# Cosine attention over chunks as a pipeline, and ternary weights made on GpSimd during the next layer's expert loop

## The chip, the cores and the metric

One core of a Trainium2 chip runs the whole program: TensorE (PE), VectorE (DVE), ScalarE (ACT), GpSimd (POOL), and SyncE (SP), which here only issues DMAs. The metric is the device time of one execution in microseconds. The engines run their own instruction lists and meet only at semaphores.

## What is computed

The program is four layers, each an attention-like sublayer and a feed-forward sublayer, over `x` of 8 x 256 tokens with 256 features, and a context of 8 x 256 tokens with 192 features. The change touches the first two sublayers and the preparation of weights for two later ones.

```
# layer 0, cosine attention: added to x
v = layernorm(x) @ Wv.T + bv            # 128 features per token
t = ctx @ Wt.T + bt
x = x + (v . t) / max(|v| * |t|, 1e-8)  # 256 x 256 for each of 8 batches

# layer 0, experts: 2 shared and 16 routed, the 4 most probable of each token gated
x = x + sum_e gate_e * (gelu(layernorm(x) @ up_e.T) @ down_e.T)

# ternary weights of layer 1 (3 matrices) and layer 3 (7 matrices)
s = max(mean|W|, 1e-5);  q = (W > s/2) - (W < -s/2)      # -1, 0 or 1
```

## The kernel before

The residual `X` stays in SBUF as 16 tiles of 128 tokens x 256 features. The cosine sublayer `l0_cosine` works in NC = 4 chunks of 512 tokens (TPC = 4 tiles, two batches). Before its loop, `layernorm` turns the normalised tokens into `XT`.

In a chunk, TensorE projects both sides into PSUM banks 0 and 1 (L494 to L496). ScalarE writes from them the squares `sq` (L527, L528) and the sides `vT`, `tT` (L529, L530). TensorE sums the squares over features by sixteen one-column instructions (L503, the squared lengths), ScalarE takes the root, VectorE the reciprocal `rn` (L541). TensorE spreads the reciprocal lengths over rows (L510) and makes the products v . t (L514). VectorE multiplies and limits the reciprocals (`lim`, L548), multiplies by the products (`cos`, L553), adds to `X` (L557) and takes the statistics of the new `X` (L156). Every one of `sq`, `vT`, `tT`, `norm`, `rn`, `lim` and `cos` is one buffer, so the order within a chunk is a chain: the lengths wait for all four of ScalarE's outputs, and the reciprocal of the next chunk stands on VectorE behind all work of the chunk before.

Into the same loop `TernaryWeights` is put, in three groups (`GROUPS`: matrices 0 and 1; 2 to 7; 8 and 9), one to each of the first three chunks. All ten matrices lie side by side in `tern_w`, 128 x 14336 fp32. ScalarE sums the absolute values (L404), TensorE spreads the sums over partitions (L409), VectorE makes the scales and thresholds (L417 to L422), GpSimd compares with the lower threshold into `below` (L427; VectorE does it for the largest matrix, `OWN = 8`), and VectorE makes `q` from the weights and `below` by one instruction per matrix (`high`, L441), in the chunk after, between the reciprocal and `lim`. SyncE stores `q` to DRAM.

The feed-forward sublayer `l0_ffn` follows. Each `nc.Block()` ends with a barrier of all engines. Its `layernorm` loads the router's weights and the attention weights of layer 1 into `K.raw` (128 x 8192 fp32, allocated after the cosine sublayer). Its `router` (L616 to L653) makes logits on TensorE; ScalarE copies `XT` to `XH` rounded, GpSimd subtracts to get `XL` (L632); VectorE then has a chain of softmax and top-4 up to the gates (L642 to L653), with the exponentials on ScalarE (L625). `small_experts` loops over 18 experts in pairs. GpSimd splits each expert's weights into a high and a low part (L725 to L729), as soon as the expert before the last is done (two buffers). A unit is an expert and a chunk, four units per expert: TensorE makes the hidden values (L744), ScalarE the gelu (L768) and its rounded copy `h_hi` (L771), VectorE the rest `h_lo` (L782), which reads two SBUF tensors, TensorE the outputs in 12 matmuls (L755 to L757), VectorE adds them gated to `X` in 4 instructions (L789), which read one tensor in PSUM and one in SBUF. TensorE runs the hidden values of the next unit ahead of the outputs of this one.

Of the kernel before, what the change touches and what calls it, by code (L numbers as in the profile page):

```python
# [26 lines left out]
ds = bass.ds  # L27

P = 128
# [332 lines left out]
class TernaryWeights:  # L362

    GROUPS = [(0, 2), (2, 8), (8, 10)]
    OWN = 8

    def __init__(self, K, ctx):
        nc, n = K.nc, TERNARY_AT[-1]
        self.K = K
        self.w = ctx.enter_context(nc.sbuf_tensor("tern_w", [P, n], F32))
        self.below, self.q = (ctx.enter_context(nc.sbuf_tensor("tern_" + x, [P, n], BF16)) for x in ("below", "q"))
        self.sums, self.thr = (ctx.enter_context(nc.sbuf_tensor("tern_" + x, [P, w], F32)) for x, w in (("sums", len(TERNARY)), ("thr", 2 * len(TERNARY))))
        self.loaded = [K.sem(f"tern_loaded{i}") for i in range(len(TERNARY))]  # L380
        self.zeroed, self.summed, self.total, self.thr_ok, self.below_ok, self.q_ok, self.stored = (
            K.sem("tern_" + x) for x in ("zeroed", "summed", "total", "thr", "below", "q", "stored"))

    def part(self, t, i):
        return t[:, TERNARY_AT[i]:TERNARY_AT[i + 1]]

    def zero_missing_rows(self, dve):

        for i, (_, rows, cols) in enumerate(TERNARY):
            if rows % P:  # L390
                dve.memset(self.w[rows % P:P, TERNARY_AT[i + 1] - cols:TERNARY_AT[i + 1]], 0.0).then_inc(self.zeroed, 1)

    def load(self, sp):
        for i, (name, rows, cols) in enumerate(TERNARY):
            load_rows(sp, self.part(self.w, i).rearrange("p (k n) -> p k n", n=cols), self.K.a[name], self.loaded[i])

    def sum(self, act, g):
        for i in range(*self.GROUPS[g]):
# [5 lines left out]
            act.activation(self.part(self.below, i), self.part(self.w, i), ACT.Abs, accum_out=self.sums[:, i:i + 1]).then_inc(self.summed, 1)  # L404

    def spread(self, pe, g):
        a, b = self.GROUPS[g]
        pe.wait_ge(self.summed, b)
        pe.matmul(self.K.bank[6][:, a:b], self.K.ones[:], self.sums[:, a:b], start=True, stop=True).then_inc(self.total, 1)  # L409

    def scales(self, dve, g):
        K, o = self.K, self.K.dve_order
        dve.wait_ge(self.total, g + 1)
        span = range(*self.GROUPS[g])
        for i in span:
            count = TERNARY[i][1] * TERNARY[i][2]
            o.mark(dve.tensor_scalar(K.wscale[:, i:i + 1], K.bank[6][:, i:i + 1], 1.0 / count, 1e-5, ALU.mult, ALU.max))  # L417
        o.wait(dve)
        a, b = self.GROUPS[g]
        n = len(TERNARY)  # L420
        dve.tensor_scalar(self.thr[:, a:b], K.wscale[:, a:b], 0.5, None, ALU.mult).then_inc(self.thr_ok, 1)
        dve.tensor_scalar(self.thr[:, n + a:n + b], K.wscale[:, a:b], -0.5, None, ALU.mult).then_inc(self.thr_ok, 1)  # L422

    def compare_low(self, eng, i, g):
        eng.wait_ge(self.thr_ok, 2 * (g + 1))
        n = len(TERNARY)
        return eng.tensor_scalar(self.part(self.below, i), self.part(self.w, i), self.thr[:, n + i:n + i + 1], None, ALU.is_lt)  # L427

    def low(self, pool, g):
        for i in range(*self.GROUPS[g]):  # L430
            if i != self.OWN:
                self.compare_low(pool, i, g).then_inc(self.below_ok, 1)

    def high(self, dve, g):
        o = self.K.dve_order
        for i in range(*self.GROUPS[g]):
            if i == self.OWN:
                o.step(dve, self.compare_low(dve, i, g))
            else:
                dve.wait_ge(self.below_ok, i + 1 - (i > self.OWN))  # L440
            dve.scalar_tensor_tensor(self.part(self.q, i), self.part(self.w, i), self.thr[:, i:i + 1], self.part(self.below, i),  # L441
                                     ALU.is_gt, ALU.subtract).then_inc(self.q_ok, 1)

    def store(self, sp):
        pieces = [(0, 2), (2, 8), (8, 9), (9, 10)]
        for a, b in pieces:
            sp.wait_ge(self.q_ok, b)
            w = slice(TERNARY_AT[a], TERNARY_AT[b])
            sp.dma_start(self.K.qweights[:, w], self.q[:, w]).then_inc(self.stored, 16)
        sp.wait_ge(self.stored, 16 * len(pieces))  # L450
# [3 lines left out]
def l0_cosine(K):  # L454
# [4 lines left out]
    nc, a, X, XT, CT, bank = K.nc, K.a, K.X, K.XT, K.CT, K.bank  # L459
    HV = 128  # L460
    with ExitStack() as ctx:
# [3 lines left out]
        vT, tT, sq = sb("vT", [P, CH]), sb("tT", [P, CH]), sb("sq", [P, 2, CH])  # L465
        norm, rn, lim, cos = sb("norm", [P, 2 * TPC]), sb("rn", [P, 2 * TPC]), sb("lim", [P, TPC, S]), sb("cos", [P, TPC, S])
# [10 lines left out]
        ternary = TernaryWeights(K, ctx)  # L477
        with nc.Block() as block:
# [5 lines left out]
        proj, sides, norms, roots, recips, dots, added = (  # L484
            K.sem("l0x_" + n) for n in ("proj", "sides", "norms", "roots", "recips", "dots", "added"))
        assert len(ternary.GROUPS) == NC - 1
        with nc.Block() as block:
            @block.tensor
            def _(pe):
                for c in range(NC):  # L490
# [8 lines left out]
                    pe.wait_ge(sides, 4 * c + 4)  # L499
# [2067 lines left out]
```

## Time and profile before

| | |
|---|---|
| median of 3 runs | 1811.87 us (1810.94 to 1814.45) |
| the profiled execution | 1816.25 us, span 1814.5 us |
| mean granted TensorE clock | 0.901 |
| busy: PE, DVE, ACT, POOL | 82%, 57%, 44%, 27% of the span |
| cosine chunks (27.1 to 106.4 us) | 79.3 us |
| layernorm and router of `l0_ffn` (106.4 to 138.1 us) | 31.7 us |
| expert loop (138.1 to 357.4 us) | 219.3 us |
| the later five sublayers | the rest, about 1457 us |

Times in the trace count from the start of the span. PEclk is the granted clock, 1.00 at 2.4 GHz and 0.50 at 1.2 GHz. A busy share over the whole span says little here, as sublayers with different limits follow each other behind barriers; the stretch has to be read.

### The profile page before, as it was taken

How to read it: one execution, taken by the hardware profiler on the slowest of the kernel's cores; microseconds unless marked ns; L12 is line 12 of the kernel's file. 1: busy time of each engine (PE TensorE's matmuls, PEld its weight loads, DVE VectorE, ACT ScalarE, POOL GpSimd, SP SyncE). 2: the span in 40 equal slices, each digit the busy share in tenths (PEclk: the TensorE clock that was granted, in tenths of full speed). 3: DMA queues.
4: the chain of work that ended last, by engine and by line, in shares of the span. 5: the costliest groups of instructions: out<-in, count | busy, mean ns of one | idle time of the engine just before them, and what ended most of it. 6: DMA issues, size and time to landing. Idle time of an engine off the chain costs nothing. (4 is left out here: it accounts for less than half of the span.)

```text
span 1814.5 us, 28465 instructions
## 1 busy us (share of the span) xinstructions
PE 1480.9 (82%) x8632; PEld 1094.7 (60%) x8632; DVE 1032.7 (57%) x2508; ACT 805.3 (44%) x1905; POOL 485.8 (27%) x717
## 2 busy tenths in 40 slices
PE   4648999789999999556599986865567739999997
PEld 3537888667777777423477764541343527667665
DVE  3766888865555555578666655545666523333332
ACT  3223444465555555456555544325546612332331
POOL 0532222263333433100264420000000442222222
PEclk9668999989999999889799999955888759999999
DMA  7141000019500000000000000013000651111110
GB/s 258 47 128 35 23 23 23 4 36 290 128 1 1 1 1 1 35 0 0 3 1 1 1 1 23 1 50 139 1 0 1 222 197 42 48 48 50 46 47 6
DMA packets 64019, 89.26 MB, mean 49 GB/s; under 512 B 7056, under 2 KB 55072, under 8 KB 62880
## 3 DMA queue, kind: packets, MB, share of 16 engines
q1 hardware_dynamic: 58624, 75.08, 13.5%
q0 software_dynamic: 5280, 12.74, 2.1%
q8 instruction: 61, 1.00, 0.2%
q14 instruction: 54, 0.44, 0.1%
HBM read 56.09 MB, written 33.54 MB: 49 GB/s over the span
## 5 line engine op out<-in xcount | busy, mean ns | idle before, releaser
L1218 POOL TENSOR_SCALAR XT<-XT,l1x_rs 128x256 f32<-128x256 f32 x256 | 117.8, 479 | 191.0 <-DVE l1x_rs L1130 191.0
L1134 DVE TENSOR_REDUCE l1x_nmax<-bank 128x2 f32<-128x512 f32 x128 | 87.4, 684 | 110.5 <-PE bank L982 110.5
L1075 ACT ACTIVATE XT<-bank,l1x_nmax 128x256 f32<-128x256 f32 x256 | 118.7, 471 | 68.5 <-DVE l1x_nmax L1134 68.5
L2227 PE MATMUL bank<-l3x_wu,XT 128*128 x312 | 142.6, 601 | 0.8 <-ACT XT L2261 0.6
L2236 PE MATMUL bank<-l3x_wd,CT 128*128 x624 | 141.4, 380 | 1.7 <-DVE CT L2304 1.6
L994 PE MATMUL bank<-ident,XT 128*128 128x128 f32 x768 | 120.7, 280 | 8.9 <-POOL XT L1218 3.3
L2236 PEld LDWEIGHTS bank<-l3x_wd,CT 128*128 128x128 f32 x624 | 115.9, 191 | 16.5 <-issue 2.6
L789 DVE SCALAR_TENSOR_TENSOR X<-bank,l0f_gates,X 128x256 f32<-128x256 f32 x288 | 118.9, 474 | 0.0
L994 PEld LDWEIGHTS bank<-ident,XT 128*128 128x128 f32 x768 | 84.3, 140 | 42.6 <-POOL XT L1218 23.6
L2271 ACT ACTIVATE CT<-bank,l3x_b 128x128 f32<-128x128 f32 x156 | 44.5, 368 | 139.3 <-PE bank L2245 139.3
L1141 DVE COPY l1x_pt<-bank 128x512 f32<-128x512 f32 x128 | 87.8, 686 | 30.2 <-PE bank L994 30.2
L2227 PEld LDWEIGHTS bank<-l3x_wu,XT 128*128 128x128 f32 x312 | 57.2, 193 | 58.4 <-issue 58.4
L768 ACT ACTIVATE l0e_h<-bank 128x512 f32<-128x512 f32 x72 | 43.0, 598 | 109.5 <-PE bank L744 109.5
L755 PE MATMUL bank<-l0e_wdhi,l0e_hhi 128*128 128x256 f32 x288 | 82.5, 287 | 2.1 <-DVE l0e_hlo L782 1.9
L782 DVE TENSOR_TENSOR l0e_hlo<-l0e_h,l0e_hhi 128x512 fp32r<-128x512 f32 x72 | 58.3, 810 | 42.7 <-ACT l0e_hhi L771 42.2
L757 PE MATMUL bank<-l0e_wdhi,l0e_hlo 128*128 128x256 f32 x288 | 81.7, 284 | 0.0
L756 PE MATMUL bank<-l0e_wdlo,l0e_hhi 128*128 128x256 f32 x288 | 81.7, 284 | 0.0
L1218 POOL TENSOR_SCALAR XT<-XT,l2x_rs 128x256 f32<-128x256 f32 x128 | 58.9, 479 | 79.3 <-DVE l2x_rs L1130 79.2
L2212 POOL DMA_INDIRECT out_x<-XT x39 | 39.2, 1005 | 144.8 <-DVE XT L2291 144.8
L2287 DVE TENSOR_TENSOR XT<-bank,CT 128x256 f32<-128x256 f32 x39 | 16.6, 425 | 103.6 <-PE bank L2236 103.6
L2296 DVE COPY CT<-bank 128x512 f32<-128x512 f32 x39 | 27.0, 692 | 84.1 <-PE bank L2227 84.1
L1075 ACT ACTIVATE XT<-bank,l2x_nmax 128x256 f32<-128x256 f32 x128 | 59.3, 471 | 33.8 <-DVE l2x_nmax L1134 33.8
(517 smaller groups left out, 3892.0 us busy)
## 6 DMA issues: line engine op xcount, KB each, us to landing
slots<-blank SPq DMA_DIRECT2D x9, 1987.5 KB, 22.8
l3x_wu<-in_L_ffn_W SPq DMA_DIRECT2D x8, 1024.0 KB
l3x_wd<-in_L_ffn_W SPq DMA_DIRECT2D x8, 1024.0 KB
XT<-slots SPq DMA_DIRECT2D x39, 132.5 KB, 2.1
qweights<-tern_q SPq DMA_DIRECT2D x3, 1024.0 KB, 3.9
l0e_wu<-in_L_ffn_upT SPq DMA_DIRECT2D x18, 128.0 KB, 2.1
l0e_wd<-in_L_ffn_downT SPq DMA_DIRECT2D x18, 128.0 KB, 2.1
X<-in_x SPq DMA_DIRECT2D x1, 2048.0 KB, 8.2
```

Of the source, the lines that this page charges most:

```text
L755: pe.matmul(y, h_hi[:, c % 2, w], wd_r[s][0][:], start=True, stop=False)
L756: pe.matmul(y, h_hi[:, c % 2, w], wd_r[s][1][:], start=False, stop=False)
L757: last = pe.matmul(y, h_lo[:, c % 2, w], wd_r[s][0][:], start=False, stop=True)
L782: dve.tensor_tensor(h_lo[:, c % 2, :], h[:, c % 2, :], h_hi[:, c % 2, :].bitcast(F32), ALU.subtract).then_inc(lo_done, 1)
L789: dve.scalar_tensor_tensor(X[:, t, :], YB[c % 2 * 2 + j // 2][:, j % 2 * D:(j % 2 + 1) * D], gates(t, pair * 2 + s), X[:, t, :], ALU.mult, ...
L994: last = pe.transpose(tp[:, c:c + P], pr[n % 3][:, i, q, kt * P:(kt + 1) * P], K.ident[:])
L1075: act.activation(pr[n % 3][:, i, q, :], sc[(2 * n + i) % 3][:, q * S:(q + 1) * S], ACT.Exp, bias=nmax[:, n % 3, i, q:q + 1], accum_out=sum ...
L1134: dve.tensor_reduce(nmax[:, n % 3, i, :], sc[(2 * n + i) % 3][:].rearrange("p (q s) -> p q s", q=QT), AX, ALU.max, negate=True).then_inc(m ...
L1141: dve.tensor_copy(pt[n % 2][:, i, :], tp[:]).then_inc(pt_ok, 1)
L1218: pool.tensor_scalar(t, t, rs[:, n % 3, i, q:q + 1], 1.0, ALU.mult, ALU.mult).then_inc(norm_ok, 1)
L2227: last = pe.matmul(up_b[half][:], xT[:, k, :], wu[:, ds(e * KD + k, 1), half * CH:(half + 1) * CH].rearrange("p a n -> p (a n)"), start=k ...
L2236: last = pe.matmul(y_b[:, 0:D], hT[:, m, :], wd[:, ds(e * HT + m, 1), :].rearrange("p a n -> p (a n)"), start=m == 0, stop=m == HT - 1)
```

## The change

`l0_cosine` becomes a pipeline: two buffers for `vT`, `tT`, `sq`, `norm`, `rn` and `cos`, products in banks 4 to 7 in turn, and on TensorE the projection of chunk c+1 before the products of chunk c, and the lengths of chunk c+1 behind them. The lengths wait for the two squares only. VectorE multiplies and adds two tiles at a time, and takes the statistics of a chunk after the next chunk's adds.

Of the ternary work only the sums of the first eight matrices (`FRONT = 8`) stay on ScalarE in this loop, with their scales at its end. Their raw weights now lie in `K.raw` (128 x 8192), the last two matrices' in `tern_back`. The comparisons are cut into 14 pieces of 1024 columns. Pieces 0 and 1 (`AHEAD = 2`) are made in `router`, the lower comparison on GpSimd before `XL`, `high` on VectorE before the logits. The other twelve are made on GpSimd alone, in three steps each (lower comparison, upper comparison, subtraction), 36 steps spread over the experts 1 to 17. The sums of the last two matrices go to ScalarE in `router`, their scales to the start of `small_experts`. The load of layer 1's attention weights and the stores of `q` go behind SyncE's expert loop.

```diff
 class TernaryWeights:
...
+    FRONT = 8
+    PIECE = 1024
+    AHEAD = 2
...
+    def low(self, pool, piece):
...
+        for i, lo, hi in self.parts(piece):
+            pool.wait_ge(self.thr_ok, 2 * (self.FRONT if i < self.FRONT else n))
+            pool.tensor_scalar(self.q[:, lo:hi], self.raw(lo, hi), self.thr[:, n + i:n + i + 1], None, ALU.is_lt).then_inc(self.below_ok, 1)
...
+    def high(self, dve, piece):
+        dve.wait_ge(self.below_ok, self.done(piece + 1))
+        for i, lo, hi in self.parts(piece):
+            dve.scalar_tensor_tensor(self.q[:, lo:hi], self.raw(lo, hi), self.thr[:, i:i + 1], self.q[:, lo:hi],
                                      ALU.is_gt, ALU.subtract).then_inc(self.q_ok, 1)
 
+    def compare_high(self, pool, piece):
+        pool.wait_ge(self.q_ok, self.done(piece))
+        for i, lo, hi in self.parts(piece):
+            start = piece * self.PIECE
+            pool.tensor_scalar(self.above[:, lo - start:hi - start], self.raw(lo, hi), self.thr[:, i:i + 1], None, ALU.is_gt).then_inc(self.above_ok, 1)
+
+    def combine(self, pool, piece):
...
+        pool.tensor_tensor(self.q[:, w], self.above[:], self.q[:, w], ALU.subtract).then_inc(self.q_ok, self.done(piece + 1) - self.done(piece))
...
+    def steps(self):
+        return 3 * (TERNARY_AT[-1] // self.PIECE - self.AHEAD)
...
@@ l0_cosine, TensorE
+                def lengths(c):
+                    pe.wait_ge(sides, 4 * c + 2)
...
+                def products(c):
                     pe.wait_ge(recips, c + 1)
                     if c:
+                        pe.wait_ge(limited, TPC * c)
...
+                project(0)
+                lengths(0)
+                for c in range(NC):
+                    if c + 1 < NC:
+                        project(c + 1)
+                    products(c)
+                    if c + 1 < NC:
+                        lengths(c + 1)
+                pe.wait_ge(roots, NC)
+                ternary.spread(pe, 0, ternary.FRONT)
...
@@ l0_cosine, ScalarE
                     if c:
+                        ternary.sum(act, c - 1, c)
...
+                ternary.sum(act, NC - 1, ternary.FRONT)
...
@@ l0_cosine, VectorE
                 for c in range(NC):
+                    dve.wait_ge(dots, c + 1)
...
+                        dve.tensor_scalar(lim[:, j, :], bank[3][:, j // 2 * S:(j // 2 + 1) * S], rn[:, c % 2, j:j + 1],
+                                          1.0 / COS_EPS, ALU.mult, ALU.min).then_inc(limited, 1)
...
+                        dve.tensor_tensor(cos[:, c % 2, 2 * b:2 * b + 2, :], bank[4 + c % 2 * 2 + b][:].rearrange("p (i s) -> p i s", s=S),
+                                          lim[:, 2 * b:2 * b + 2, :], ALU.mult).then_inc(cos_ok, 1)
+                    if c + 1 < NC:
+                        recip(c + 1)
...
+                        dve.tensor_tensor(xt, xt, cos[:, c % 2, 2 * b:2 * b + 2, :], ALU.add).then_inc(added, 1)
+                    if c:
+                        stats(c - 1)
+                ternary.scales(dve, 0, ternary.FRONT)
+                stats(NC - 1)
...
@@ router
+                if ternary:
+                    ternary.sum(act, ternary.FRONT, len(TERNARY))
...
+                    if ternary:
+                        for piece in range(ternary.AHEAD):
+                            ternary.low(pool, piece)
...
+                if ternary:
+                    for piece in range(ternary.AHEAD):
+                        ternary.high(dve, piece)
...
@@ small_experts
+                sp.wait_ge(ternary.q_ok, ternary.done(8))
+                if K.last >= 2:
+                    load_attention_weights(K, sp, "l1x")
+                ternary.store(sp)
...
-                for s in range(2):
-                    split(0, s)
-                with pool.Fori(1, E // 2) as pair:
-                    for s in range(2):
-                        split(pair, s)
+                for e in range(E):
+                    split(e)
+                    if e:
+                        for n in range((e - 1) * ternary.steps() // (E - 1), e * ternary.steps() // (E - 1)):
+                            ternary.step(pool, n)
```

## Rows read from the trace of the kernel before

**Rows 1.** Windows: stretch, length, busy PE, PEld, DVE, ACT, POOL, granted clock, DMA

```profile
27.00:31.10 4.10, 3.87 (x8) 1.35 (x8) 0.00 (x0) 3.98 (x5) 0.00 (x0) 1.00 1.07 384
48.10:51.80 3.70, 3.57 (x16) 3.49 (x16) 0.00 (x1) 0.05 (x1) 3.59 (x1) 0.50 0.01 4
57.70:61.60 3.90, 3.84 (x9) 1.30 (x9) 3.90 (x2) 0.02 (x1) 1.38 (x1) 1.00 0.01 2
90.00:106.40 16.40, 2.75 (x10) 1.99 (x8) 16.24 (x19) 0.00 (x0) 5.72 (x1) 0.60 0.23 96
119.00:138.10 19.10, 10.76 (x64) 10.68 (x64) 7.28 (x60) 5.41 (x4) 8.99 (x2) 0.59 0.23 63
149.80:348.00 198.20, 198.07 (x1259) 177.65 (x1257) 166.77 (x351) 94.68 (x148) 51.73 (x64) 1.00 0.06 19
```

**Rows 2.** Timeline, cosine chunks on PE and ACT: start, length, engine, line, operation

```profile
37.45 2.07 PE L510 MATMUL bank<-ident,l0x_rn 128*128 128x128 f32 x8 [0.50 <-DVE l0x_rn L541]
39.31 2.47 PE L514 MATMUL bank<-l0x_tT,l0x_vT 128*128 128x256 f32 x8
48.14 3.57 PE L503 MATMUL bank<-ones,l0x_sq 128*128 128x1 f32 x16 [2.51 <-ACT l0x_tT L530]
54.09 3.60 PE L514 MATMUL bank<-l0x_tT,l0x_vT 128*128 128x256 f32 x8
61.58 0.69 ACT L527 ACTIVATE l0x_sq<-bank,l0x_bv 128x512 f32<-128x512 f32 x1 [4.17 <-PE bank L496]
```

**Rows 3.** Timeline, VectorE in the last chunk

```profile
88.07 2.35 DVE L427 TENSOR_SCALAR tern_below<-tern_w,tern_thr 128x4096 bf16<-128x4096 f32 x1
...
90.46 10.07 DVE L441 SCALAR_TENSOR_TENSOR tern_q<-tern_w,tern_thr,tern_below 128x4096 bf16<-128x4096 f32 x2
100.46 1.65 DVE L548 TENSOR_SCALAR l0x_lim<-bank,l0x_rn 128x256 f32<-128x256 f32 x4
102.14 1.42 DVE L553 TENSOR_TENSOR l0x_cos<-bank,l0x_lim 128x256 f32<-128x256 f32 x4
103.59 1.43 DVE L557 TENSOR_TENSOR X<-X,l0x_cos 128x256 f32<-128x256 f32 x4
104.94 1.40 DVE L156 BATCH_NORM_STATS2 stats<-X 128x6 f32<-128x256 f32 x4
```

**Rows 4.** Timelines, ternary comparisons of VectorE and GpSimd side by side

```profile
53.69 5.81 DVE L441 SCALAR_TENSOR_TENSOR tern_q<-tern_w,tern_thr,tern_below 128x2048 bf16<-128x2048 f32 x1 [1.52 <-POOL tern_below L427]
53.65 5.43 POOL L427 TENSOR_SCALAR tern_below<-tern_w,tern_thr 128x2048 bf16<-128x2048 f32 x1
59.42 2.34 DVE L441 SCALAR_TENSOR_TENSOR tern_q<-tern_w,tern_thr,tern_below 128x2048 bf16<-128x2048 f32 x1
78.03 1.17 DVE L441 SCALAR_TENSOR_TENSOR tern_q<-tern_w,tern_thr,tern_below 128x512 bf16<-128x512 f32 x1 [0.37 <-POOL tern_below L427]
77.97 1.56 POOL L427 TENSOR_SCALAR tern_below<-tern_w,tern_thr 128x512 bf16<-128x512 f32 x1
```

**Rows 5.** Router: GpSimd's second subtraction, VectorE's first with two SBUF inputs

```profile
125.50 4.51 POOL L632 TENSOR_TENSOR l0f_xl<-XT,l0f_xh 128x2048 fp32r<-128x2048 f32 x1
130.75 0.42 DVE L646 TENSOR_TENSOR l0r_ex<-l0r_lg,l0r_mx 128x256 f32<-128x256 f32 x1
```

**Rows 6.** Timelines, expert loop, GpSimd and VectorE

```profile
182.15 1.10 POOL L725 TENSOR_TENSOR l0e_wuhi<-l0e_wu,zero 128x256 fp32r<-128x256 f32 x1 [8.03 <-PE bank L757]
184.72 0.74 POOL L729 TENSOR_TENSOR l0e_wdlo<-l0e_wd,l0e_wdhi 128x256 fp32r<-128x256 f32 x1
184.79 1.22 DVE L782 TENSOR_TENSOR l0e_hlo<-l0e_h,l0e_hhi 128x512 fp32r<-128x512 f32 x1 [0.56 <-ACT l0e_hhi L771]
187.61 0.69 DVE L782 TENSOR_TENSOR l0e_hlo<-l0e_h,l0e_hhi 128x512 fp32r<-128x512 f32 x1
329.48 1.10 POOL L725 TENSOR_TENSOR l0e_wuhi<-l0e_wu,zero 128x256 fp32r<-128x256 f32 x1 [8.03 <-PE bank L757]
```

**Rows 7.** Groups of 27 to 107 us: ScalarE's sum of the largest matrix

```profile
L404 ACT ACTIVATE tern_below<-tern_w 128x4096 bf16<-128x4096 f32 x1 | 3.6, 3608 | 0.0
```

More of the change, by code:

```diff
@@ L424, in compare_low @@
[L424 to L441, printed above, removed]
-                                     ALU.is_gt, ALU.subtract).then_inc(self.q_ok, 1)
+            w = slice(TERNARY_AT[i], TERNARY_AT[i + 1])
@@ L444, in store, with step @@
+    def step(self, pool, n):
+        piece = self.AHEAD + n // 3
+        if n % 3 == 0:
+            self.low(pool, piece)
+        elif n % 3 == 1:
+            self.compare_high(pool, piece)
+        else:
+            self.combine(pool, piece)
+    def steps(self):
+        return 3 * (TERNARY_AT[-1] // self.PIECE - self.AHEAD)
     def store(self, sp):
[L445 to L448, printed above, removed]
+        for a, b in ((0, 8), (8, 14)):
+            sp.wait_ge(self.q_ok, self.done(b))
+            w = slice(a * self.PIECE, b * self.PIECE)
@@ L489, in _, with project @@
             def _(pe):
-                for c in range(NC):
+                def project(c):
                     if c:
@@ L561, in _ @@
-                    if c < NC - 1:
-                        ternary.scales(dve, c)
-            @block.gpsimd
-            def _(pool):
-                for g in range(NC - 1):
-                    ternary.low(pool, g)
-            @block.sync
-            def _(sp):
-                ternary.store(sp)
+                        dve.tensor_scalar(lim[:, j, :], bank[3][:, j // 2 * S:(j // 2 + 1) * S], rn[:, c % 2, j:j + 1],
+                                          1.0 / COS_EPS, ALU.mult, ALU.min).then_inc(limited, 1)
@@ L777, in _ @@
                 dve.sem_inc(lo_done, 2)
+                ternary.scales(dve, ternary.FRONT, len(TERNARY))
                 def rest(pair, s, c, n):
@@ L2502, in _ @@
                     sp.wait_ge(K.ctx_loaded, 48)
-        for sublayer in stages[first:min(last + 1, 1)]:
-            sublayer(K)
         with nc.sbuf_tensor("raw", [P, 8 * 1024], F32) as raw:
             K.raw = raw
-            for sublayer in stages[max(first, 1):min(last + 1, 5)]:
+            with ExitStack() as weights:
+                K.ternary = TernaryWeights(K, weights)
+                for sublayer in stages[first:min(last + 1, 2)]:
+                    sublayer(K)
+            for sublayer in stages[max(first, 2):min(last + 1, 5)]:
                 sublayer(K)
```

171 lines of the change are left out of this document (90 added, 81 removed).

## The prediction

> **What bounds the kernel now.** The barriers between sublayers make the whole span's shares useless, so I first read windows cut at the barriers and phases [rows 1]. They show three regimes. In the cosine chunks nothing is busy throughout: in 27.00:31.10 TensorE projects and VectorE has nothing, in 90.00:106.40 VectorE works for 16.24 of 16.40 us and TensorE for 2.75. In the router every engine mostly waits for one chain. In the expert loop TensorE is busy for 198.07 of 198.20 us at a clock of 1.00, and VectorE for 166.77. So a microsecond on VectorE is worth one in the first, and nothing in the loop until its spare (16%) is gone.
>
> The timeline then tells the order inside a chunk [rows 2, 3]: projection, squares, lengths, reciprocal, products, VectorE. In the last chunk the products have long been possible when VectorE is still on ternary weights: 88.07 to 100.46, 12.4 us, and only then `lim`. The stage ends at 104.94 + 1.40 = 106.3.
>
> **Cosine, what sets the end after.** VectorE loses all comparisons and keeps per chunk 1.65 + 1.42 + 1.43 + 1.40 = 5.9 us and a reciprocal [rows 3]. TensorE needs more, so I sum along it [rows 1, 2]. A projection takes 3.9 us (3.84 to 3.87 busy, at clock 1.00). Lengths take 3.6 at half clock (3.57), which I round to 3.5, since the clock may be higher. Products take 39.31 - 37.45 = 1.9 for the spreading, and 2.5 (clock rising) to 3.6 (half) for the rest: 4.4 to 5.5. The first projection still ends at 31.0; two squares of at most 0.7 each free the lengths at 32.3 (before, they waited for four outputs); lengths end at 35.8. Three rounds of projection, products and lengths follow, then 0.5 for root and reciprocal (the idle before L510), and the last products. With 4.4: 35.8 + 3 x 11.8 + 0.5 + 4.4 = 76.1. With 5.5: 35.8 + 3 x 12.9 + 0.5 + 5.5 = 80.5. If the three later projections ran wholly at the half clock they'd take 3.9 more each: 92.2. No row shows a projection that follows lengths directly; the clock was 0.50 during lengths at 48.10 and 1.00 in the projection behind products at 57.70. I take 79, for some of each.
>
> Behind the last products VectorE has `lim`, `cos`, add, the third chunk's statistics, the scales and the fourth's statistics. That is 1.65 + 1.42 + 1.43 + 2 x 1.40 = 7.3 [rows 3], and the ten scale instructions on a few columns. Their nearest row is 0.42 for 256 columns [rows 5], which bounds them by 0 and 4.2; they are hundreds of times smaller, so near the low end: 0.7. Two tiles per instruction save at most two starts each. Tail 8.0, end 87.0. ScalarE's work per chunk (four outputs, one sum) lies under TensorE's 12 us, and the last sums (matrices 3 to 7, together half of the largest one's 3.6 us, and four more starts [rows 7]) beside the last products. Gain 106.3 - 87.0 = **19.3 us**, between 23 (76.1 + 7.3) and 5.5 (92.2 + 8.6).
>
> **Router.** Put before `XL` on GpSimd: two comparisons of 1024 columns. 512 columns took 1.56 us and 2048 took 5.43 [rows 4], 2.52 ns per column and 0.27 fixed, so 2.85 each, 5.7 together. They start at the block's start, 119.0. Behind them `XL` is 2 x 4.5 [rows 5], so GpSimd ends at 133.7 and not at 130.0. VectorE's two `high` (half of 2.34 each, 1.2, alone) lie under its wait for the logits at 129.8, if they are let in. But VectorE's chain then has L646 at 130.75, with two SBUF inputs, where GpSimd's second subtraction used to be over and now runs. How two such instructions meet the trace shows [rows 4, 6]: whoever started first goes on, and the other gains little. VectorE's `h_lo` at 184.79, behind L729 at 184.72, takes 1.22 instead of 0.69; GpSimd's L725 takes 1.10 behind an `h_lo`. L729 held the other for 0.53 of its 0.74 us, a two-input instruction for 0.7 to all of its length. So L646 waits until 133.3 to 133.7, or to 135 where a `high` has got between the subtractions: +2.2 to +4. The bound below is 0 (it gets in before the second subtraction). I take **+3.2**. ScalarE's added sums (3.6 [rows 7] and half of it, 5.4) hide: it is busy 5.41 us in that window [rows 1], and 10.8 in all still fits before the exponential at 131.2. The start of the next block moves with this chain; the spread and scales there lie under the wait for the first weights.
>
> **Expert loop.** GpSimd's added work: twelve pieces, two comparisons of 2.85 and a subtraction. A two-input one is 4.51 for 2048 columns, 0.74 for 256 [rows 5, 6], so 2.4. That is 97 us, with 1.6 for pieces 6 and 7, which are cut at the matrices' borders: 99 us over 17 experts, 5.8 each. An expert takes (329.48 - 182.15) / 13 = 11.33 us, and GpSimd waits for 8.03 of them [rows 6]. It fits. Two gaps have three steps, 8.1; what they run over is taken from the split's double buffer, needed a whole expert later. So GpSimd is no bound.
>
> What counts is `h_lo`, the only VectorE instruction of the loop with two SBUF inputs (the adds, L789, read one). VectorE has 11.33 x 0.16 = 1.8 us spare per expert, 0.45 per unit, and one `h_lo` of four already takes 0.53 longer with TensorE still full [rows 1, 6]. A comparison holds the other engine for only part of its time: behind one of 512 columns a VectorE instruction took 1.17 where 0.6 is its own, +0.55 of 1.56; behind one of 2048, 5.81 and not 2.34, +3.5 of 5.43 [rows 4]. For 1024 that makes 1.3 to 1.7 from the step's start. Counted from the split's start at 182.15, `h_lo` comes at 2.6, 5.5 and 8.3; the first step starts at 3.3 to 3.8, the second near 6.7. So `h_lo` arrives 1.6 to 2 us into a step and finds the way free or nearly so; behind a subtraction (held for 1.7 of 2.4) it waits 0.2 to 0.4. That stays within 0.45. I take 0.1 per expert, **+1.5**; bounds 0, and the rival below.
>
> The Trainium skill speaks against this part: "SBUF — State Buffer", section Who interferes with whom, says that the one which starts second is fully blocked until the first has finished. The trace disagrees with it in size: by that rule the instruction at 53.69 would have taken 5.4 + 2.3 = 7.7 us, and took 5.81 [rows 4]. What the rule would make of the loop is rival B.
>
> **Hidden moves.** Layer 1's weights and the stores now stand behind SyncE's loop. Its last expert load follows the split of expert 15, about two experts before 329.48, so near 310; the 4.2 MB of `raw` at the 384 GB/s of the first window are 11 us, landed by 322, and attention starts after 357. GpSimd's last three steps end at 329.5 + 3.3 + 8.1 = 341, and the last store (1.5 MB, 4 us) near 345, while TensorE is still busy at 348 [rows 1, 6]. Nothing; without that cover it would cost what exceeds 357.
>
> **Sum.** -19.3 + 3.2 + 1.5 = -14.6 us. The profiled execution took 1816.25 (span 1814.5 and 1.75 around it), which gives 1801.65; the median of the runs is 4.4 below that execution, so **1797 us** for a median. The forecast's own range is 1793 to 1804.
>
> **Rivals.**
> A, the clock. The one-column lengths keep TensorE at 1.2 GHz through each projection. For it: the lengths of 48.10:51.80 ran at 0.50. Against: TensorE no longer idles, and the projection of 57.70:61.60 was at 1.00 right behind products [rows 1]. End of the stage at 92.2 + 8 = 100.2, gain 6.1, net -1.4: 1810.5.
> B, the opposite side: `h_lo` waits to the end of each GpSimd step. Steps at 3.8 to 6.65 and 7.3 to 10.2 delay the `h_lo` at 5.5 and 8.9 by 1.2 and 1.3. Per expert that is 2.5 less two spares of 0.45, 1.6; or, if VectorE makes use of all its spare, 2.5 - 1.8 = 0.7. The middle, 1.15 x 17 = 19.6, with +4.5 in the router: net +4.8, 1816.7. It decides from (19.3 - 4.5) / 17 = 0.87 us per expert. For it: the skill's rule, and the `h_lo` at 184.79, held for most of L729 [rows 6]. Against: 5.81 where the rule makes 7.7 [rows 4].
> C, more gain: TensorE at full clock throughout and L646 not held: -23 + 0 + 0.5, 1789.4.
>
> **Chances.** The forecast 0.74, A 0.08, B 0.10, C 0.08. A change under 0.2%, 3.6 us, can't be told from none in this kernel. A lies within it; B is slower in a bit over half of its cases, the others are faster. Faster 0.84, same 0.09, slower 0.07. The range of 1791 to 1809 leaves out B's upper part, half of C and little else.
>
> **What would show it.** Cosine chunks ending near 87 (over 95: clock or a wait I missed), with TensorE busy throughout 36 to 75; VectorE without L441's kind there; projections of 3.9. L646 of 3 us or more in the router, and GpSimd's subtractions up to 134. In the loop 11.3 to 11.5 us per expert, and `h_lo` with a mean under 1.1 us (before, 1.22 once per expert and 0.69 otherwise [rows 6]); a mean over 1.5, and TensorE waiting for it, means B. Attention's start waiting for `raw` would be a cost that I put at nothing. The prediction is wrong if the stage's order on TensorE leaves gaps: each is paid four times.

## The result, and the profile after

The changed kernel takes 1785.83 us (median of 4 executions, 1784.32 to 1787.35) against 1811.4 of the kernel before in the same comparison (1810.43 to 1814.45): a ratio of 0.9842, 95% interval 0.982 to 0.9864. It is 25.6 us faster; 14.6 were forecast. A later comparison on one chip gave 1786.96 against 1809.94, ratio 0.9872 (0.9851 to 0.9893), so the gain is 23 to 26 us. Either time lies beyond the low end of the predicted range, 1791.

The profiled execution took 1784.32 us, with a span of 1782.6 and a mean granted clock of 0.911. First its windows, cut as in [rows 1]: one whole round of the pipeline, the end of the cosine stage, the router, the expert loop.

```profile
core 0: us, PE busy (x) PEld busy (x) DVE busy (x) ACT busy (x) POOL busy (x), PEclk, DMA share, GB/s
45.80:54.00 8.20, 8.20 (x42) 5.52 (x41) 4.09 (x10) 4.46 (x8) 0.00 (x0) 1.00 0.01 2
62.40:76.00 13.60, 4.69 (x19) 4.03 (x18) 11.25 (x36) 2.81 (x11) 0.00 (x0) 0.69 0.00 1
76.70:110.70 34.00, 17.07 (x96) 16.14 (x96) 24.52 (x85) 15.69 (x17) 15.75 (x5) 0.60 0.01 1
110.70:332.90 222.20, 208.25 (x1298) 185.39 (x1298) 183.01 (x382) 99.04 (x153) 161.29 (x115) 0.96 0.17 57
```

The first row is what the change is about: in the cosine stage TensorE is now busy for all of a round, at a clock of 1.00, and VectorE for half of it. Where a chunk before went through 3.57 us of lengths at half clock [rows 1], TensorE's timeline of the changed kernel shows this (L510 to L512 project, L522 the lengths, L530 and L537 the products):

```profile
start us, us, engine line op out<-in xcount [idle before <-releaser]
32.46 2.61 PE L522 MATMUL bank<-ones,l0x_sq 128*128 128x1 f32 x16 [1.36 <-ACT l0x_sq L559]
34.94 3.76 PE L510 MATMUL bank<-XT,l0x_wv 128*128 128x512 f32 x4
...
41.39 1.16 PE L530 MATMUL bank<-ident,l0x_rn 128*128 128x128 f32 x8
42.38 1.89 PE L537 MATMUL bank<-l0x_tT,l0x_vT 128*128 128x256 f32 x8
44.11 1.84 PE L522 MATMUL bank<-ones,l0x_sq 128*128 128x1 f32 x16
...
60.58 1.84 PE L522 MATMUL bank<-ones,l0x_sq 128*128 128x1 f32 x16
63.80 1.67 PE L530 MATMUL bank<-ident,l0x_rn 128*128 128x128 f32 x8 [1.38 <-DVE l0x_rn L577]
65.26 3.09 PE L537 MATMUL bank<-l0x_tT,l0x_vT 128*128 128x256 f32 x8
```

The reader is to see two things. The same sixteen one-column instructions that took 3.57 us take 1.84, and the eight instructions of the products 1.89, not 3.60 [rows 2]. And the engine is slow again in just two places, each behind a wait: after 1.36 us of idle time the lengths take 2.61 and the next projection 6.45 (34.94 to 41.39, at a granted clock of 0.58) for its usual 3.9, and after 1.38 us the last products take 3.09. (The profile shows each fp32 matmul of the program as two instructions: e4's three extra matmuls appear as x6.)

VectorE's end of the stage, and then its part of the router with GpSimd's instructions beside it:

```profile
63.55 0.19 DVE L577 RECIPROCAL l0x_rn<-l0x_norm 128x8 f32<-128x8 f32 x1
...
68.39 1.66 DVE L590 TENSOR_SCALAR l0x_lim<-bank,l0x_rn 128x256 f32<-128x256 f32 x4 [2.17 <-PE bank L537]
...
74.53 1.40 DVE L156 BATCH_NORM_STATS2 stats<-X 128x6 f32<-128x256 f32 x4
...
94.25 5.55 DVE L434 SCALAR_TENSOR_TENSOR tern_q<-raw,tern_thr,tern_q 128x1024 bf16<-128x1024 f32 x1 [0.69 <-POOL tern_q L429]
...
100.63 3.81 DVE L689 TENSOR_TENSOR l0r_ex<-l0r_lg,l0r_mx 128x256 f32<-128x256 f32 x1
```
```profile
88.54 5.68 POOL L429 TENSOR_SCALAR tern_q<-raw,tern_thr 128x1024 bf16<-128x1024 f32 x2 [0.42 <-SPq L646]
94.19 9.97 POOL L672 TENSOR_TENSOR l0f_xl<-XT,l0f_xh 128x2048 fp32r<-128x2048 f32 x2
```

The stage ends at 75.93, and not at 106.3. In the router L434 (the second `high`) came 0.06 us behind the start of the first subtraction of L672 and got through only after that had ended (98.7); the second subtraction (5.47 us of the two's 9.97) then ran to 94.19 + 9.97 = 104.16, and L689, which was L646 and took 0.42 [rows 5], came while it ran and ended at 104.44.

Then the groups of the expert loop, 110.7 to 332.9, and below them the group of `h_lo` before:

```profile
line engine op names shapes xcount | busy us, mean ns | idle before us <-releasers
L830 DVE TENSOR_TENSOR l0e_hlo<-l0e_h,l0e_hhi 128x512 fp32r<-128x512 f32 x72 | 63.7, 885 | 36.6 <-ACT l0e_hhi L818 36.4
...
L801 PEld LDWEIGHTS bank<-l0e_wdhi,l0e_hhi 128*128 128x128 f32 x288 | 54.8, 190 | 9.9 <-DVE l0e_hlo L830 4.5 <-issue 2.9
...
L447 POOL TENSOR_TENSOR tern_q<-tern_above,tern_q 128x1024 bf16<-128x1024 bf16 x12 | 28.0, 2337 | 1.1 <-POOL tern_above L441 0.2
```
```profile
L782 DVE TENSOR_TENSOR l0e_hlo<-l0e_h,l0e_hhi 128x512 fp32r<-128x512 f32 x72 | 58.3, 810 | 42.7 <-ACT l0e_hhi L771 42.2
```

`h_lo` has a mean of 885 ns and had 810 before, 5.4 us in the whole loop. VectorE still stands idle for 36.6 us ahead of it, and TensorE's weight loads wait for it for 4.5 us (3.5 before).

By the starts of the sublayers (VectorE's first statistics instruction) the two profiled executions compare so:

| | before | after | part's difference |
|---|---|---|---|
| `l0_ffn` starts | 107.3 | 76.7 | -30.6 (cosine) |
| gates made (L653, now L696) | 137.4 | 110.7 | +3.9 (layernorm, router) |
| layer 1 attention starts | 358.5 | 332.9 | +1.1 (loop) |
| layer 2 feed-forward starts | 1094.2 | 1069.0 | +0.4 |
| layer 3 attention starts | 1210.2 | 1180.0 | -5.0 |
| end of the span | 1814.5 | 1782.6 | -1.7 |

Up to layer 1 this is -25.6, the whole difference of the medians in the first comparison (23.0 in the later one). The last two rows are code that the change doesn't touch. They are what one execution differs from another there: a second profiled execution of the changed kernel had layer 2's feed-forward part at 1066.7 to 1182.8, 116.1 us, where the first had 111.0 and the kernel before 116.0. So the sum has to be read up to layer 1.

### The profile page after: what moved, and what is told of

Read it like the earlier page. It is cut to its first block and busy times, and to the rows that moved or that the text cites. A ratio compares the mean times of both kernels' runs of the same rounds, so it can differ in the third digit from the quotient of the medians.

```text
span 1782.6 us, 28456 instructions
## 1 busy us (share of the span) xinstructions
PE 1464.7 (82%) x8630; PEld 1079.6 (61%) x8630; DVE 1019.5 (57%) x2481; ACT 805.4 (45%) x1905; POOL 565.0 (32%) x752
## 5 line engine op out<-in xcount | busy, mean ns | idle before, releaser
L830 DVE TENSOR_TENSOR l0e_hlo<-l0e_h,l0e_hhi 128x512 fp32r<-128x512 f32 x72 | 63.7, 885 | 36.6 <-ACT l0e_hhi L818 36.4
L2256 POOL DMA_INDIRECT XT<-out_x,XT x39 | 40.5, 1039 | 104.6 <-DMA out_x<-XT 95.8
## 6 DMA issues: line engine op xcount, KB each, us to landing
tern_back<-in_L_xattn_W_f1T SPq DMA_DIRECT2D x1, 2048.0 KB, 10.7
```

What stands on the lines that cost most here:

```text
L830: dve.tensor_tensor(h_lo[:, c % 2, :], h[:, c % 2, :], h_hi[:, c % 2, :].bitcast(F32), ALU.subtract).then_inc(lo_done, 1)
```

## The experiments

Two theories of the 11 us that the cosine stage gained beyond the forecast stood against each other. The clock theory: the times of the lengths and products before were half-clock times, and the clock was half because the old order let TensorE wait; without the waits they halve. The neighbour theory: TensorE's short instructions were slowed by the ternary work that ran beside them on VectorE and GpSimd. And of GpSimd's steps in the expert loop it was open whether they cost little because they hold VectorE only in part, or because the schedule kept them apart. E5 to e8 ran on a chip on which the kernel before took 1823.62 us (e1 to e4: 1812.47; e9 to e11: 1809.94), so ratios are compared, or differences within a trace.

**E1, the old order of the chunks, with the ternary work moved.** `l0_cosine` keeps its old loop and single buffers; the ternary work is where the change puts it.

```diff
-                    pe.wait_ge(sides, 4 * c + 2)
+                    pe.wait_ge(sides, 4 * c + 4)
...
-                project(0)
-                lengths(0)
```


> The changed kernel with the old chunk loop (single buffers, the lengths behind all four outputs, one tile per add), and the ternary work moved as in the change. Theory 1, the clock: what made the cosine stage 11 us shorter than predicted is that TensorE, kept busy by the pipeline, ran the lengths and products at 2.4 GHz (lengths 1.7 us, products 2.6 us per chunk, where I had priced 3.5 and 4.4 to 5.5 from half-clock rows). Then here, with TensorE idle between steps, the lengths still take about 3.4 us and the products 4.4 or more, a chunk 14.7 us, and the stage ends near 93 us (75.9 in the changed kernel): total 1803 us. Rival, theory 2, the neighbours: they took long because VectorE and GpSimd worked on the ternary weights beside them. Then lengths are at 1.8 and products at 2.7 here too, a chunk takes 12 us, the stage ends near 82 us: total 1792 us.

Measured 1800.9 us, ratio 0.9938 (0.9907 to 0.9969). Its timeline of TensorE in the second chunk (L517 the lengths, L524 and L528 the products), and the windows of lengths and products:

```profile
46.61 3.58 PE L517 MATMUL bank<-ones,l0x_sq 128*128 128x1 f32 x16 [2.51 <-ACT l0x_tT L543]
50.69 2.07 PE L524 MATMUL bank<-ident,l0x_rn 128*128 128x128 f32 x8 [0.50 <-DVE l0x_rn L555]
52.56 3.62 PE L528 MATMUL bank<-l0x_tT,l0x_vT 128*128 128x256 f32 x8
```
```profile
46.60:50.20 3.60, 3.58 (x16) 3.49 (x16) 0.00 (x0) 0.00 (x0) 0.00 (x0) 0.50 0.00 0
50.70:56.00 5.30, 5.30 (x17) 4.58 (x18) 0.00 (x0) 1.59 (x2) 0.00 (x0) 0.50 0.01 3
```

VectorE and GpSimd show 0.00 in both rows, and the lengths still take 3.58 and the products 3.62 at a clock of 0.50. The neighbour theory falls. The waits of 2.51 and 0.50 us stand in front of the slow instructions. The clock doesn't always fall within such a wait: in the first chunk the lengths behind the same 2.51 us took 1.95, at 0.97, and only the spreading behind them was slow (2.08).

**E2, the pipeline, with the ternary work where it was.** The other half of the change alone, built on the kernel before: the new loop, with the old `TernaryWeights` in it (the diff is against the kernel before). Its sums move from bank 6, which the products now need, to bank 2 of the lengths, so the lengths also wait for the thresholds.

```diff
-        pe.matmul(self.K.bank[6][:, a:b], self.K.ones[:], self.sums[:, a:b], start=True, stop=True).then_inc(self.total, 1)
+        pe.matmul(self.K.bank[2][:, 16 + a:16 + b], self.K.ones[:], self.sums[:, a:b], start=True, stop=True).then_inc(self.total, 1)
...
+                def lengths(c):
+                    pe.wait_ge(sides, 4 * c + 2)
...
+                    pe.wait_ge(ternary.thr_ok, 2 * max(c, 1))
```


> The kernel before with the pipelined chunk loop and nothing of the ternary work moved (three groups, on ScalarE, GpSimd and VectorE in the cosine stage; the sums spread one place earlier, since bank 2 is shared with the lengths). VectorE then has 23 us of cosine and 28 us of ternary work from about 43 us on, with waits for GpSimd between: the stage ends at 92 to 98 us, 8 to 14 us before the old one, total 1798 to 1803. If the two parts of the change were independent, this and the run with the old loop would add up to the whole 25.6 us; I expect them to fall short of it by 4 us or more, since each alone leaves the other's chain as the bound. Theory 1: the lengths are near 2 us wherever TensorE has not waited, 3.4 behind a wait. Theory 2: they stay above 3 us, as the ternary work is beside them.

Measured 1798.9 us, ratio 0.9932 (0.9905 to 0.9958). It answers the two theories from the other side. The lengths at 50.91 took 1.84 us at a clock of 1.00, with GpSimd on its ternary comparison for all of that time (1.70 of 1.70 us in 50.91:52.61); the last ones, behind a wait of 4.45 us for the thresholds, took 2.75. Layer 0's feed-forward part starts at 95.8 (-11.5). The medians' two halves are 11.6 and 13.6 us, 25.2 together and near the whole's 25.6, but each has an interval of some 10 us from end to end. The traces, up to layer 1, are sharper: -9.0 (349.5 for 358.5) and -10.7 (347.8), 19.7 together for 25.6, as the expectation said (4 us or more short). In the cosine stage alone the halves give 13.3 and 11.5 of the 30.6. So the two help each other by 6 us there: without the moved ternary work VectorE is the bound (busy almost without a gap from 57.4 to 93.2), and without the pipeline TensorE's waits are. How much of the 6 us is due to this run's added wait for the thresholds isn't separated.

**E3, no pieces in the router.** All 14 pieces are made in the expert loop.

```diff
-    AHEAD = 2
+    AHEAD = 0
```


> The changed kernel with AHEAD = 0: all 14 pieces in the expert loop, none in the router. The router's 3.7 us are, by my prediction's step, VectorE's L689 waiting for GpSimd's second subtraction (3.81 us, 0.42 before). Then L689 falls back to 0.42 and the router by 3.4 us; the loop has 42 steps for 36, GpSimd about 10.5 of 11.33 us busy per expert, and pays 0 to 0.5 us: total 1782.5 us. Rival: the subtraction isn't what holds it, and the total stays at 1786; or GpSimd gets past 11.33 us per expert and the loop is 5 us or more longer, total 1788 or more.

Measured 1782.8 us as the median of four (one took 2056.96; the other three have a median of 1781.73), ratio 0.9827 (0.9788 to 0.9865) without that one. The interval overlaps the changed kernel's, so the gain is read from the trace:

```profile
98.75 0.43 DVE L689 TENSOR_TENSOR l0r_ex<-l0r_lg,l0r_mx 128x256 f32<-128x256 f32 x1
```

L689 takes 0.43 us again, and from the start of the part to the gates there are 30.1 us, as before the change; the loop took 221.7 with six more steps. So the two pieces account for the router's +3.9, of which 3.4 are L689. The length of this part also varies by itself: e7 and e11, likewise without pieces, took 32.5 and 31.2, with logits of 13.0 and 12.1 us where e3 has 10.7.

**E4, filler that keeps TensorE busy in the two waits.** Three extra matmuls of 256 columns ahead of the first lengths and of the last products, into banks that nothing reads.

```diff
                 project(0)
+                warm(7, 3)
                 lengths(0)
...
+                    else:
+                        pe.wait_ge(sides, 4 * NC)
+                        warm(0, 3)
```


> The changed kernel with three fp32 matmuls of 256 columns on data that is there, before the first lengths (TensorE waits 1.36 us there) and before the last products (1.38 us); their results are used by nothing. Theory 1: the wait before the first lengths brings the clock down, so that the second projection takes 6.45 us instead of 3.8, and the wait before the last products stretches these (4.2 for 2.6 us). Filled, both run at the full clock: 2.6 and 1.4 us less, total 1782 us. Theory 2, or a clock that falls for another reason (the lengths themselves): nothing gained, 1786 us.

Measured 1780.64 us, ratio 0.9824 (0.9786 to 0.9863). That interval too overlaps the changed kernel's; the trace is sharper. Its timeline of TensorE (L542 is the filler), and the windows over the first two projections and over the second filler with the last products:

```profile
31.70 1.56 PE L542 MATMUL bank<-XT,ident 128*128 128x256 f32 x6
33.12 1.95 PE L522 MATMUL bank<-ones,l0x_sq 128*128 128x1 f32 x16
34.93 1.96 PE L510 MATMUL bank<-XT,l0x_wv 128*128 128x512 f32 x4
...
61.14 1.16 PE L530 MATMUL bank<-ident,l0x_rn 128*128 128x128 f32 x8
62.14 1.89 PE L537 MATMUL bank<-l0x_tT,l0x_vT 128*128 128x256 f32 x8
```
```profile
27.90:45.00 17.10, 17.09 (x75) 10.62 (x76) 3.54 (x9) 7.08 (x12) 0.00 (x0) 1.00 0.46 178
59.60:64.00 4.40, 4.40 (x26) 3.71 (x25) 3.96 (x10) 2.83 (x12) 0.00 (x0) 1.00 0.01 2
```

With the waits filled, the second projection takes 3.8 us and not 6.45, the last products 1.89 and not 3.09, and the clock is 1.00 in both windows. From the first projection to the next part there are 44.5 us, where the changed kernel has 49.5: 2.6 from the projection, 0.7 from the first lengths and 1.7 from the last spreading and products. The same work on the same data became faster by giving the engine more to do.

**E5, larger pieces.** Pieces of 2048 columns, one of them in the router; 6 in the loop, 18 steps of about twice the length.

```diff
-    PIECE = 1024
-    AHEAD = 2
+    PIECE = 2048
+    AHEAD = 1
```


> The changed kernel with pieces of 2048 columns (one in the router, six in the expert loop, 18 steps over 17 experts). It asks how long a GpSimd comparison holds a VectorE instruction with two SBUF inputs. Theory hold: for part of its length, 0.55 us at 512 columns, 3.5 at 2048. Each h_lo that falls into the first 3.5 us of a 5.4 us step is then late by 1 to 3 us, more than the 0.45 us per unit that VectorE has to spare; one or two of the four per expert do. The mean of h_lo rises from 0.89 to 1.3 us or more, the loop by 0.5 to 1 us per expert, 9 to 17 us: total 1794 to 1803. Rival: it is not the length of the instruction that counts (a fair split between the two engines): the same GpSimd time costs the same, h_lo stays near 0.9 and the total at 1786. The router has the same columns before XL, so 3 to 4 us as in the changed kernel.

Measured 1820.06 us, ratio 0.9977 (0.9958 to 0.9997). The loop takes 249.4 us, 27.2 more than with pieces of 1024, and `h_lo` 92.7 us in all where it took 63.7. The timelines of GpSimd and, below, of VectorE's `h_lo` show how:

```profile
153.06 4.55 POOL L447 TENSOR_TENSOR tern_q<-tern_above,tern_q 128x2048 bf16<-128x2048 bf16 x1
...
166.12 5.88 POOL L429 TENSOR_SCALAR tern_q<-raw,tern_thr 128x2048 bf16<-128x2048 f32 x1
```
```profile
155.24 2.92 DVE L830 TENSOR_TENSOR l0e_hlo<-l0e_h,l0e_hhi 128x512 fp32r<-128x512 f32 x1
...
168.28 2.54 DVE L830 TENSOR_TENSOR l0e_hlo<-l0e_h,l0e_hhi 128x512 fp32r<-128x512 f32 x1
```

An `h_lo` takes 0.69 alone. The one at 155.24 ended at 158.16, so it was let in at about 157.5, as the two-input L447 ended (157.61). The one at 168.28 ended at 170.82 and was let in at about 170.1, 4.0 us into a comparison of 5.88. So the partial hold that the prediction read off the comparisons is real, as is the full one of two-input instructions. The cost is 1.6 us per expert, and well over what was expected. It comes through `h_lo`: TensorE's weight loads waited for it for 27.1 us (4.5 in the changed kernel), while GpSimd itself still had 3.5 to 5.3 us to spare per expert in the stretch shown. The same total of GpSimd work costs little in 36 steps of about 3 us (1.7 us, e6) and takes the change's gain away in 18 of 4.5 to 6.

The Trainium skill ("SBUF — State Buffer", section Who interferes with whom) has the second instruction fully blocked for the whole of the first. For the two-input L447 this trace agrees (let in at 157.5, end 157.61); for the comparison it doesn't (let in 1.9 us before its end).

**E6, no steps in the loop.** The 36 steps are left out, so the ternary values of pieces 2 to 13 are not computed.

```diff
-                        for n in range((e - 1) * ternary.steps() // (E - 1), e * ternary.steps() // (E - 1)):
-                            ternary.step(pool, n)
+                        pass
+                pool.sem_inc(ternary.q_ok, ternary.done(14) - ternary.done(ternary.AHEAD))
```


> The changed kernel with the 36 steps left out of the expert loop: the ternary values of pieces 2 to 13 are not computed, and later layers read what lay there; the same number of instructions follows. It prices the steps. By my prediction they cost 1.5 us, by the trace of the changed kernel the loop is 1.1 us longer than before: total 1784.7, h_lo back to a mean of 0.81. Rival B (h_lo held to the end of each step) would have them cost 20 us; then 1766.

Measured 1799.05 us, ratio 0.9847 (0.9808 to 0.9887). The loop takes 220.5 us and `h_lo` has a mean of 812 ns, as before the change:

```profile
L830 DVE TENSOR_TENSOR l0e_hlo<-l0e_h,l0e_hhi 128x512 fp32r<-128x512 f32 x72 | 58.4, 812 | 40.3 <-ACT l0e_hhi L818 40.0
```

So the steps cost 1.7 us in the loop (one execution each; the loop before the change, without steps too, took 221.1), and rival B's 19.6 are refuted. The ratio, too, is the changed kernel's within its interval.

**E7, both improvements together.** `AHEAD = 0` and the filler.

> The version that the runs so far point to: the changed kernel with all pieces in the expert loop and the fillers before the first lengths and the last products. If the two gains are of separate stages they add: -4.4 in router and loop, -5 in the cosine stage, total 1776.5 us. Rival: GpSimd at 10.6 of 11.33 us per expert leaves no room, or the clock comes down later instead; then 1780.

Measured 1789.8 us, ratio 0.9807 (0.9771 to 0.9843). On the scale of 1811.9 that is 1776.9, as expected, but the interval is 13 us wide; in the trace attention of layer 1 starts at 325.6, 7.3 us earlier than in the changed kernel and not 8.9. E11 repeats it.

**E8, the old order with filler.** As e1, with six matmuls of 256 columns between the projection and the lengths of every chunk. If the waits make the clock fall, filling them must help the old order too.

```diff
+                    warm(pe, 6)
                     pe.wait_ge(sides, 4 * c + 4)
```


> The run with the old chunk loop and the ternary work moved, with six fp32 matmuls of 256 columns in each chunk between projection and lengths, where TensorE waits 2.5 us for ScalarE; nothing else is overlapped. Theory 1, the clock: filled, the lengths take 1.8 us and the products 2.6 in all four chunks (3.5 and 4.4 to 5.5 in three of four without filler), so the stage ends some 9 to 12 us sooner, at 81 to 84 us where it was 93.2: total 1789 to 1792. Theory 2, that the pipeline's order makes them cheap and not the clock: the stage stays at 93, total 1801.

Measured 1803.59 us, ratio 0.9883 (0.9846 to 0.992). TensorE in its first two chunks behind the filler (L521 lengths, L528 and L532 products):

```profile
33.73 1.84 PE L521 MATMUL bank<-ones,l0x_sq 128*128 128x1 f32 x16
36.08 1.16 PE L528 MATMUL bank<-ident,l0x_rn 128*128 128x128 f32 x8 [0.51 <-DVE l0x_rn L559]
37.07 3.33 PE L532 MATMUL bank<-l0x_tT,l0x_vT 128*128 128x256 f32 x8
...
46.91 1.84 PE L521 MATMUL bank<-ones,l0x_sq 128*128 128x1 f32 x16
49.25 1.16 PE L528 MATMUL bank<-ident,l0x_rn 128*128 128x128 f32 x8 [0.50 <-DVE l0x_rn L559]
50.25 1.89 PE L532 MATMUL bank<-l0x_tT,l0x_vT 128*128 128x256 f32 x8
```

The lengths take 1.84 in all four chunks, with no other change; the stage is 7.9 us shorter than in e1. Summed over the chunks the lengths give 4.8 us, the spreading 3.2 and the products 0.6; the projections and the fillers' own ends take 0.7 back. It is less than the 9 to 12 expected, because the products fell to half clock all the same in three of four chunks (3.33, 3.14, 3.58). That they didn't in the second, behind the same idle time of 0.50, is not explained by these runs.

**E9, filler in the router too.** E7, and more. The transposes of the layernorm (6.65 us in e7) and the router's logits (13.02) run mostly at half clock. Four fillers stand ahead of the transposes, four among the logits.

```diff
+                    if ternary and t % 4 == 0:
+                        pe.matmul(bank[7][:, 0:S], K.ident[:], K.CT[:, 0, 0:S], start=True, stop=True)
```


> As the version with filler and without pieces in the router, plus four filler matmuls (fp32, 256 columns) ahead of the layernorm's transposes and four among the router's logits. In that version the transposes took 6.65 us and the logits 13.02, at a granted clock of 0.50 to 0.71. If the clock follows what TensorE did just before, here too, and the logits are on the chain that ends the router, the logits take 7 to 8 us and the expert loop starts 4 to 6 us earlier: 1771 to 1773 on the scale of 1811.9. If the pause ahead of the transposes is too long for four matmuls to bridge, or GpSimd's subtractions (9.0 us) end the chain instead, the time is within 1 us of the version without this filler.

Measured 1778.89 us, ratio 0.9835 (0.981 to 0.9859), against 1777.14 without it on the same chip: no gain. TensorE in the layernorm and the router (L272, L660 filler):

```profile
71.74 3.61 PE L272 MATMUL bank<-CT,ident 128*128 128x256 f32 x8 [8.28 <-PEq L94]
75.37 1.09 PE L278 MATMUL bank<-ident,ln0f_xn 128*128 128x128 f32 x8
...
82.70 1.85 PE L662 MATMUL bank<-l0f_wr,XT 128*128 128x16 f32 x16
...
84.92 3.05 PE L662 MATMUL bank<-l0f_wr,XT 128*128 128x16 f32 x16
...
93.07 3.43 PE L662 MATMUL bank<-l0f_wr,XT 128*128 128x16 f32 x16
```

The windows over the logits, with filler (e9) and, below, without (e11):

```profile
80.00:88.00 8.00, 6.50 (x43) 6.19 (x43) 0.11 (x1) 7.06 (x6) 3.96 (x2) 0.83 0.00 1
88.00:96.00 8.00, 8.00 (x35) 7.64 (x35) 0.00 (x0) 4.66 (x5) 5.22 (x2) 0.50 0.00 0
```
```profile
80.00:88.00 8.00, 6.15 (x43) 5.71 (x42) 0.89 (x4) 6.63 (x7) 2.59 (x2) 0.84 0.01 3
88.00:96.00 8.00, 7.64 (x36) 7.53 (x36) 0.32 (x1) 6.03 (x5) 6.59 (x2) 0.50 0.00 0
```

The first quarter of the logits took 1.85 us, the second 3.05 and the others 3.43. But that is not the filler's doing: without it the logits too began at full clock and went on at half (1.00 in 83.56:85.41, 0.51 in 85.41:88.46), so the filler among them did not change the clock and only took its own time, 14.3 us for all where e11 has 12.1. Ahead of the transposes it did help: all four groups of these ran in 1.1 us, and the logits began 10.5 us behind the part's start for e11's 11.4. Together that is 1.2 us lost. In the last window TensorE was busy throughout and still at 0.50, so half clock is not only met behind a wait; why it fell there these runs don't show.

**E10 and e11, the changed kernel and the version of e7 again, on one chip with e9.**

> The changed kernel unaltered, on the same chip as the two filled versions, so that they can be compared with it directly. Ratio to the kernel before again 0.984.

> The version without pieces in the router and with filler in the cosine stage, again, beside the changed kernel on the same chip. If its two gains (3.9 and 5.0 us by the traces) are real, it lies 7 to 9 us below the changed kernel here; if the 1777 worked out from the first run was chance, within 3 us.

Measured 1786.96 us (1784.1 to 1791.14, 5 executions), ratio 0.9872, for the changed kernel, and 1777.14 us (1774.65 to 1778.47, 5), ratio 0.9815 (0.9797 to 0.9834), for the version with both improvements. It is 9.8 us faster and no execution overlaps. The traces agree with 7.3 of that: attention of layer 1 starts at 324.8 and at 332.1, 4.4 us from the cosine stage, 2.7 from the router and 0.2 from the loop. Of the 8.9 us expected from the two parts, most of what is missing did not come in the router, which took 31.2 us and not e3's 30.1, with logits of 12.1 us for 10.7.

## Why the prediction was right and wrong

The forecast of "faster" held, and so did the mechanisms named for the router and the loop. The size did not, and one term carries the whole miss:

| term | predicted | measured | off by |
|---|---|---|---|
| cosine stage, its end | 87.0, gain 19.3 | 75.9, gain 30.4 | 11.1 |
| layernorm and router | +3.2 | +3.9 | 0.7 |
| expert loop | +1.5 | +1.1 | 0.4 |
| moved loads and stores | 0 | 0 | 0 |
| sum | -14.6 | -25.6 | 11.0 |

- **TensorE's sum in the cosine stage is the step that failed.** It put the last products' end at 79, from 3.5 us for the lengths and 4.4 to 5.5 for the products in each of three rounds of 11.8 to 12.9. The rounds took 8.23 us, but for the first (10.88), and the last products ended at 68.35. The lengths were 1.84 and the spreading and products 2.7 (41.39 to 44.11). All those prices came from [rows 1, 2], where the granted clock was 0.50 or rising. The prediction wrote the half clock down beside them and took it along into a schedule in which the waits that e1, e4 and e8 show ahead of it are gone. Projections, priced at full clock, were right (3.9) where no wait stood ahead. Two losses that its sum didn't have, 2.6 us in the second projection and 0.9 of the wait below, made the miss smaller than the error in these prices.
- **The wait ahead of the last products** was put at 0.5 us, for root and reciprocal, and was 1.38. The lengths ended at 62.42 and the root at 62.63, but VectorE made the reciprocal at 63.55 only, since in the new order it stands behind `lim` and `cos` of the chunk before.
- **Even rival C was too short.** It called itself full clock throughout and still summed rounds of 11.8, which hold lengths at 3.5 us. With 1.8 and 2.8 in it the round would have been 8.5, the end of the last products 31.0 + 1.3 + 1.8 + 3 x 8.5 + 0.5 + 2.8 = 62.9, plus 7.3 behind it: 70.2. Measured was 75.9, the difference being mostly the second projection (+2.6), the slow last products (+1.7), the wait of 1.38 for 0.5 ahead of them (+0.9) and the first lengths (+0.8). E4 removes all of these but the wait's length; its stage ends at 71.6 and began 0.7 us later, so 70.9 by the same count.
- **Rival A, the clock**, had the right resource and the wrong sign. One projection of three did run near half clock, as it says; but its cause was the 1.36 us wait ahead of the first lengths, not the one-column lengths themselves, since the two later projections behind lengths were at 1.00 and e4's second one, with the wait filled, took 3.8.
- **The tail** of 8.0 us was 7.5 (68.39 to 75.93); the ten scale instructions took 0.9.
- **The router** went as worked out: L689 took 3.81 us, 3.39 over its own, held by the second subtraction, and a `high` had got in between the two, the case that the prediction priced at the upper end. E3 shows that without the two pieces it is gone.
- **The expert loop** went as worked out: +1.1 for +1.5, the steps themselves 1.7 (e6). `h_lo`'s mean of 885 ns lies under the 1.1 us named as the bound, with TensorE's waits up by 1 us. The partial hold by comparisons, on which this rested, is measured by e5 (4.0 of 5.88 us). What the argument did not see is how near the edge it stood: with steps of 4.5 to 6 us the cost is 27 us.
- **Hidden moves**: the loads of layer 1's weights were issued from 285.5 on and the stores from 290.2 to 315.7, the last landing 5.0 us behind, all ahead of 332.9, and attention reads `raw` from 334.2 on without a wait for it.

## What to carry to other kernels

Before a duration on TensorE is carried from one schedule to another, read the granted clock beside it and ask what would lift it: a short matmul behind a wait may have been timed at half clock, and removing the wait can then pay twice, once for the wait and once for what runs behind it. When GpSimd work is laid beside VectorE instructions that read two SBUF tensors, cut it so finely that the VectorE instruction arrives when a step is nearly over (steps of about 3 us cost 1.7 us here, steps of 4.5 to 6 us 27 more), and put none on a serial chain like a router. A pipeline's first and last wait are worth a few dead matmuls, if long work stands behind them.

## What the runs showed of the hardware

- The same sixteen one-column fp32 instructions took 1.84 us at a granted clock of 1.00 and 3.58 at 0.50, and eight of 128x256 took 1.89 and 3.62: small matmuls follow the clock almost in full, by a factor of 1.9.
- A wait as short as 1.36 us was followed by half-clock work that outlasted it: 2.6 us lost in the 3.9 us projection behind the lengths. The clock doesn't follow a wait strictly: behind the same 0.50 us the products took 1.89 us in one chunk of e8 and 3.14 to 3.58 in the others. Filling two waits of 2.7 us in all made the stage 5.0 us shorter (e4).
- Three fp32 matmuls of 256 columns in a wait of 1.4 us kept the clock at 1.00 for the work behind it (e4). Among the router's 16-column matmuls filler changed nothing: 0.83 and 0.50 in two windows of 8 us with it (e9), 0.84 and 0.50 without (e11), TensorE being busy for all of the second with it.
- A one-input comparison of 2048 columns on GpSimd (5.88 us) let a two-input instruction of VectorE in only 4.0 us after its own start, and a two-input one (4.55 us) only at its end (e5).
- Unchanged code of one part (layer 2's feed-forward) took 111.0 us in one execution and 116.1 in another of the same kernel, so a difference of 5 us between single traces of a part of that length is no finding. The 5.0 us of e4 lie in a stage of 50 us, instruction by instruction, and e11 against e10 shows 4.4 of them again.
